# Late x1 rows fetched batch by batch in an AdaLN, feed-forward and mixture-of-experts kernel

## The reference, cut to what matters

```python
x = x + ffn0(adaln(x, cond))          # ternary weights, 8-bit activations, D_FF = 2048
y = causal_conv(x, taps)              # depthwise, 16 taps per channel (taps = cond)
logits = y @ Wr                       # 8 experts
w, sel = top_k(logits, 2)
w = softmax(w)
x = x + sum over e of gate[..., e] * (y @ We[e] + be[e])
```

## Time and profile before

| | |
|---|---|
| median of three runs | 834.71 us (832.91 to 834.76) |
| the profiled execution's own time | 831.19 us |
| its span | 829.2 us, 13313 instructions |
| TensorE matmul busy | 730.0 us, 88% |
| VectorE, ScalarE, GpSimd busy | 532.6, 436.9, 499.5 us |
| TensorE's mean granted clock | 0.948 of 2.4 GHz |

### The profile page before, as it was taken

One profiled execution on the slowest core, in us unless ns is written; L12 is line 12 of the kernel. 1 busy time (PEld: TensorE's weight loads), 2 busy tenths in 40 slices (PEclk: granted clock), 3 DMA queues, 4 the chain that ended last, 5 costly groups with the idle time before them and its releaser, 6 DMA issues.

```text
span 829.2 us, 13313 instructions
## 1 busy us (share of the span) xinstructions
PE 730.0 (88%) x3808; PEld 479.1 (58%) x3808; DVE 532.6 (64%) x765; ACT 436.9 (53%) x721; POOL 499.5 (60%) x760
## 2 busy tenths in 40 slices
PE   1754679999999999999999789984689999999995
PEld 0111235555555555655555479983568888888884
DVE  2467989889888888848975433684364544444442
ACT  2055466777777877658777423571343333333332
POOL 1036888777777787747862320011568888788773
PEclk9986899999999999989999988997689999999998
DMA  9985135656667766737656457799978989888883
GB/s 357 387 303 184 32 74 100 130 124 154 151 141 166 140 150 140 152 75 147 139 101 133 88 106 65 198 242 286 291 156 154 161 159 163 161 157 160 154 156 41
DMA packets 225049, 132.25 MB, mean 159 GB/s; under 512 B 182402, under 2 KB 186498, under 8 KB 223826
## 3 DMA queue, kind: packets, MB, share of 16 engines
q1 hardware_dynamic: 206866, 91.65, 46.5%
q0 software_dynamic: 15904, 35.48, 23.2%
q10 hardware_dynamic: 2208, 4.28, 1.7%
HBM read 74.44 MB, written 37.78 MB: 135 GB/s over the span
## 4 chain that ended last, share of the span: by engine, by line
PE 74%; DMA 9%; SPq 7%; DVE 4%; issue 3%; POOL 2%; ACT 2%; POOLq 0%; DVEq 0%; ACTq 0%
PE PS L1761 21%; PE PS L1595 12%; PE PS L1607 12%; PE PS L1618 12%; PE PS L1672 6%; PE PS L1743 3%; PE PS L1639 3%; SPq L424 3%; DMA z_scratch<-ZS 2%; SPq L509 2%; DMA WRT<-in_Wr 2%; PE PS L1648 2%; PE PS L1630 1%; DMA QyT<-Qy 1%; DMA X<-in_x 1%
## 5 line engine op out<-in xcount | busy, mean ns | idle before, releaser
L1761 PE MATMUL PS<-W,ZH 128*128 x568 | 187.6, 412 | 6.4 <-DVE W L1357 6.3
L1595 PE MATMUL PS<-W,QyT 128*128 128x512 bf16 x512 | 126.0, 391 | 26.4 <-DMA QyT<-Qy 16.2
L881 POOL DMA_INDIRECT out_x<-YS,IDS x71 | 114.1, 1606 | 43.7 <-issue 21.2
L1105 ACT ACTIVATE YS<-YS,SG 128x512 f32<-128x512 f32 x71 | 51.4, 724 | 150.5 <-DVE YS L1520 150.5
L1607 PE MATMUL PS<-W,QyT 128*128 128x512 bf16 x512 | 122.3, 382 | 0.0
L1761 PEld LDWEIGHTS PS<-W,ZH 128*128 128x128 f32 x568 | 104.8, 194 | 26.6 <-issue 7.7
L872 POOL DMA_INDIRECT ZR<-z_scratch,IDG x71 | 74.0, 1042 | 72.2 <-DVE IDG L1467 32.4
L1618 PE MATMUL PS<-W,QT 128*128 128x512 bf16 x512 | 116.8, 381 | 0.0
L1761 PE MATMUL PS<-W,ZL 128*128 x284 | 114.0, 401 | 0.0
L1499 DVE TENSOR_TENSOR ZL<-PS,ZH 128x512 fp32r<-128x512 f32 x71 | 49.1, 692 | 98.1 <-ACT ZH L1091 98.1
L942 ACT ACTIVATE SG<-PS,sm 128x1024 f32<-128x1024 f32 x64 | 71.3, 1114 | 60.1 <-PE PS L1595 60.1
(11 more groups left out here) (249 smaller groups left out, 1110.8 us busy)
## 6 DMA issues: line engine op xcount, KB each, us to landing
X<-in_x SPq DMA_DIRECT2D x32, 256.0 KB, 10.0
out_x<-X SPq DMA_DIRECT2D x32, 256.0 KB, 2.5
WRAW<-in_We SPq DMA_DIRECT2D x32, 256.0 KB, 9.0
ST<-out_x SPq DMA_DIRECT2D x28, 256.0 KB, 3.5
XR<-in_x SPq DMA_DIRECT2D x20, 256.0 KB, 3.5
z_scratch<-ZS SPq DMA_DIRECT2D x1, 4112.0 KB, 17.9
z_scratch<-ZS ACTq DMA_DIRECT2D x1, 4112.0 KB, 18.7
stage<-in_w1T SPq DMA_DIRECT2D x4, 1024.0 KB, 7.9
```

Of the source, the lines that this page charges most:

```text
L881: pool.indirect_dma_start(x1_d, bass.IndirectOffsetOnAxis(IDS[:, m:m + 1].bitcast(U32), 0), YS[m % UN][:], None, bounds_check=TOK - 1, oob ...
L1595: i = nc.tensor.matmul(GP[:, a, :], QyT[t][:, k, :], W12[:, k, o:o + CH], start=(k == 0), stop=(k == KD - 1))
L1761: x = nc.tensor.matmul(bank[i], zz[i % 2][:, k, :], W2[:, bass.ds(q, 1), part, k, :].rearrange("p o d -> p (o d)"), start=(k == 0 and n == ...
```

## The change

`stage_late(b)` now fetches one batch: b = 8 and 9 in stage 28, 10 and 11 in stage 29, 12 in stage 30, 13 in stage 31, each behind `stage_xw` and ahead of the g store. It has a counter of its own, stl_in. GpSimd copies STL into XW in stage 32, between the memset of BD 12:28 and that of BD 60:64, and no longer behind its constants of the routing. STL moves over PJ, so a batch waits for the last sums that read PJ (sum_done); STB moves over the Y tiles and, in its second use, over ION. The two last tap pieces are one, 44 to 64. The exponential stands behind the ZS copy of group 11. The waits on bd_zero are counted anew. The words "z stored whole" in the change's title have no line in the diff; `store_z` is as it was.

```diff
--- before.py
+++ after.py
@@ -144,8 +144,8 @@
         a += D // 2 * 5
         GAM = place("GAM", a, [P, D])
         BET = place("BET", a + D, [P, D])
-        STL = place("STL", a_s + 3 * D, [P, BH - 2, CB, NI - IL])
-        STB = place("STB", a_s + 5 * D, [P, CB, NI])
+        STL = place("STL", a_s + 5 * D, [P, BH - 2, CB, NI - IL])
+        STB = place("STB", a_h + OB * ZP, [P, CB, NI])
         TMP = place("TMP", a + 2 * D, [P, FF], I16)
         TMPB = place("TMPB", a + 2 * D, [P, FF], BF16)
         a += 2 * D + FF // 2
@@ -300,6 +300,7 @@
         pj_in = [sem(f"pj_in{t}") for t in range(2)]
         x1_out = [sem(f"x1_out{t}") for t in range(2)]
         st_in, xw_copied, xw_v = [sem(f"st_in{i}") for i in range(2)], sem("xw_copied"), sem("xw_v")
+        stl_in = sem("stl_in")
         z_out, z_free = [sem(f"z_out{h}") for h in range(2)], sem("z_free")
         ext_in = sem("ext_in")
 
@@ -343,7 +344,7 @@
         trz_done, zh_done, zl_done, exp_done, ys_done = (sem(n) for n in ("trz_done", "zh_done", "zl_done", "exp_done", "ys_done"))
 
         VM2 = 25
-        PIECES = [(0, 4), (4, 12), (12, IA), (IA, IB), (IB, IC), (IC, NI)]
+        PIECES = [(0, 4), (4, 12), (12, IA), (IA, IB), (IB, NI)]
         LATE_XW = 2 * (B - 2)
 
         def group(r):
@@ -486,13 +487,12 @@
                 sp.dma_start(ST[c][:], bass.AP(x1_d.tensor, b * S * D + c * (CB // 2) * OB * D,
                                                [[NI, P], [OB * D, CB // 2], [1, NI]])).then_inc(st_in[c], 16)
 
-            def stage_late():
-
-                sp.wait_ge(down_done, NT)
+            def stage_late(b):
+
+                sp.wait_ge(sum_done, NT - TB)
                 for t in range(TB):
-                    sp.wait_ge(x1_out[t], 16 * (B - 2))
-                sp.dma_start(STL[:].rearrange("p b k i -> p (b k) i"),
-                             bass.AP(x1_d.tensor, BH * S * D + IL, [[NI, P], [OB * D, (BH - 2) * CB], [1, NI - IL]])).then_inc(st_in[0], 16)
+                    sp.wait_ge(x1_out[t], 16 * b + 16)
+                sp.dma_start(STL[:, b - BH], bass.AP(x1_d.tensor, b * S * D + IL, [[NI, P], [OB * D, CB], [1, NI - IL]])).then_inc(stl_in, 16)
 
             def stage_last(b):
 
@@ -500,6 +500,8 @@
                     sp.wait_ge(x1_out[t], 16 * b + 16)
                 if b == B - 1:
                     sp.wait_ge(xw_v, 1)
+                else:
+                    sp.wait_ge(yint_done, NT)
                 sp.dma_start(STB[:], bass.AP(x1_d.tensor, b * S * D, [[NI, P], [OB * D, CB], [1, NI]])).then_inc(st_in[1], 16)
 
             def load_bd(i):
@@ -575,6 +577,8 @@
                     load_xr(s + 5)
                 if 4 <= s < NT:
                     stage_xw(s - 4)
+                for b in {28: (8, 9), 29: (10, 11), 30: (12,), 31: (13,)}.get(s, ()):
+                    stage_late(b)
                 if tile(s - 4) and s - 4 < NT - 1:
                     store_g(s - 4)
                 if 6 <= s <= 32 and s % TB == 0 and s != 22:
@@ -588,22 +592,16 @@
             pipeline(stage)
 
             load_gs(B - 2)
-            sp.wait_ge(bd_zero, 5)
+            sp.wait_ge(bd_zero, 6)
             sp.wait_ge(bd_zero_v, 3)
             sp.wait_ge(bd_in[0], 16 * NJ)
             load_bd(3)
             load_gs(B - 1)
             stage_last(B - 1)
-            sp.wait_ge(bd_zero, 6)
+            sp.wait_ge(bd_zero, 7)
             sp.wait_ge(bd_zero_v, 4)
             sp.wait_ge(bd_in[1], 16 * NJ)
             load_bd(4)
-            sp.wait_ge(bd_zero, 4)
-            sp.wait_ge(bd_in[2], 16 * NJ)
-            load_bd(5)
-            stage_late()
-            sp.wait_ge(x1t_done, NT)
-
             def load_expert(e):
 
                 if e >= E // 2:
@@ -796,6 +794,8 @@
                 if s == NT:
                     pool.wait_ge(hint_done, NT)
                     pool.memset(BD[:, 12:IA], 0.0).then_inc(bd_zero, 1)
+                    pool.wait_ge(stl_in, 16 * (BH - 2))
+                    pool.tensor_copy(XW[:, 1, IL:NI, 1:1 + CB, 0:BH - 2], STL[:].rearrange("p b k i -> p i k b")).then_inc(bd_zero, 1)
                     pool.wait_ge(xw_copied, LATE_XW)
                     pool.memset(XW[:, 1, IL:NI, 0, :], 0.0)
                     pool.memset(BD[:, IC:NI], 0.0).then_inc(bd_zero, 1)
@@ -856,8 +856,6 @@
             pool.memset(STEP[:, 5:6], 2.0)
             pool.memset(STEP[:, 7:8], 0.0).then_inc(route_p, 1)
 
-            pool.wait_ge(st_in[0], 16 * (LATE_XW // 2 + 1))
-            pool.tensor_copy(XW[:, 1, IL:NI, 1:1 + CB, 0:BH - 2], STL[:].rearrange("p b k i -> p i k b")).then_inc(bd_zero, 1)
             pool.wait_ge(ext_in, 48)
             pool.wait_ge(slots_done, 2)
 
@@ -1071,8 +1069,9 @@
                     copy_lg(1)
                 if r == 10:
                     act.wait_ge(route_v, 4)
+                    act.wait_ge(xw_v, 2)
                     nc.scalar.copy(ION[:], IOSB[:].rearrange("p (m o) -> p m o", o=1).broadcast_to([P, P, CC])).then_inc(route_e, 1)
-                if r == 12:
+                if r == 11:
                     act.wait_ge(route_v, VM2)
                     nc.scalar.activation(EX[:], M2[:], ACT.Exp).then_inc(route_e, 1)
                 if r in (20, 22, 24, 26):
@@ -1431,8 +1430,6 @@
                     dve.wait_ge(tab_done, q - 1)
                     dve.wait_ge(num_done, NUMS * (q - 1))
 
-                if q == 0:
-                    dve.wait_ge(bd_zero, 7)
                 nc.vector.tensor_tensor(BOX[h][:], over(IOSB, 0, MT), along(MTB, q, MT), ALU.is_equal).then_inc(boh_done, 1)
                 dve.wait_ge(boh_done, 2 * q + 1)
                 nc.vector.tensor_scalar(BOH[h][:, :, 1, :], BOX[h][:], PIDX[h], None, ALU.mult).then_inc(boh_done, 1)
@@ -1661,7 +1658,7 @@
                 if r == NG:
                     pe.wait_ge(xw_copied, LATE_XW)
                     pe.wait_ge(xw_v, 2)
-                    pe.wait_ge(bd_zero, 7)
+                    pe.wait_ge(bd_zero, 5)
                 if r < NG:
                     pe.wait_ge(bd_in[piece_of(g) % 3], 16 * NJ * (1 + piece_of(g) // 3))
                 if r >= 4:
```

## The result

| | before | after |
|---|---|---|
| median of 20 runs | 833.94 us (831.17 to 836.13) | 835.37 us (833.50 to 838.69) |
| ratio, after to before | | 1.0025, 95% interval 1.0015 to 1.0034 |
| the profiled execution | 831.19 us, span 829.2 | 838.69 us, span 836.6 |
| TensorE busy, mean granted clock | 730.0 us, 0.948 | 731.8 us, 0.939 |

A forecast was written before the change was run, and what follows sets the result against it. SyncE's queue, without a gap from 463.25, was taken to bound the hand-over to the convolution. Only stage 31 cost anything, +0.86 us, all other terms 0: 834.71 + 0.86 = 835.6 us, range 832.3 to 837.2.

The forecast's parts named there:

- Rival A: SyncE, stage 31: the issue behind a 2048-run load is stretched and moves the tap pieces, 835.6 us; chance 0.56.
- The surplus: SyncE's queue: extra time that each new 2048-run load puts on the issue behind it, taken as 0.95 us.
- the QyT row: SyncE, stage 28: QyT transpose behind a GS load takes 2.16 us to issue, against 1.21 the stage before.
- The cover: SyncE, stage 31: its wait ahead of piece 0 for VectorE's memset of BD 0 to 4, 0.72 us, absorbs added issuing.
- One sign of being wrong: TensorE, convolution: the forecast is wrong if the time from group 3 to the last group changes by over 0.5 us.
- The covers: Slack or idle time on the queues and engines that was to hold the change's other parts at cost 0.
- stages 28 to 30: SyncE's queue: added loads fit the slack between a transpose and its use a stage later; cost 0.
- the copy on GpSimd: GpSimd, stage 32: the 1.60 us copy fits ahead of 14 us of idle time; cost 0.
- the merged pieces: SyncE, last tap pieces: 8 issues fewer save 6 us of queue that nobody takes up; gives 0.
- Rival B: SyncE, stage 31: no stretch, or it falls into the wait; 0.63 us against 0.72 of cover, 834.7 us; chance 0.18.
- Rival D: SyncE, stage 31: queue stands behind batch 13 until it lands, +2.6 us, 837.3 us; or a counter holds an engine; chance 0.13.
- Rival C: TensorE, group 16: usually waits for the late load's copy; removing that wait makes it faster, down to 832.1 us; chance 0.13.

## Why the prediction was right

*The mechanism.* Rival A, the forecast, is what happens: a stretched issue behind batch 13, then tap pieces, groups 1 and 3, and the end. Taking that batch away takes the loss away, and leaving out the other parts does not.

*The sizes.* The forecast was +0.86 us and the median 835.6; measured are +1.4 by medians, +2.1 by the ratio (interval 1.3 to 2.8), and a median of 835.37. That the median came within 0.3 us is luck: that of before was taken 0.8 us too high, and the step 0.6 to 1.2 us too low. The surplus was taken as 0.95 us from the QyT row and is 1.20 (1.84 less 0.64). The cover, taken as 0.72 us, was too large by 0.09: without any wait SyncE still has a gap of 0.09 between the g store and piece 0. With 0.66 for the load and its gaps that gives 0.66 + 1.20 - 0.63 = 1.23, against 1.24 measured for the shift of piece 0. The rest was not in the sum at all. Over the four profiles with one batch in stage 31 group 3 starts at 28.04 us behind the memset in the mean, over the five with none and SyncE issuing alone at 26.48: +1.55 us. The column "rest" gives 82.15 against 80.49, +1.66, and here no profile of the one kind reaches those of the other (81.86 to 82.50, and 80.28 to 80.61). This lies in the intervals of all three kernels timed with one batch there.

*Where the sum stopped too early.* The prediction let piece 2 and group 3 move by what piece 0 moves. The start of piece 2 does (+1.22 us in the mean), its end does not (+2.15). Here are, in the kernel before, the last issue of piece 2 and the g store behind it; then, after, the sixth and the last issue of piece 2:

```profile
486.69 0.61 SPq L509 DMA_DIRECT2D BD<-taps_scratch  x1
...
487.98 0.96 SPq L519 DMA_DIRECT2D g_scratch<-GT  x1
```

```profile
488.37 0.61 SPq L511 DMA_DIRECT2D BD<-taps_scratch  x1
...
489.94 1.50 SPq L511 DMA_DIRECT2D BD<-taps_scratch  x1
```

In all nine profiles one issue that starts 23.3 to 25.0 us behind the memset is stretched by 0.4 to 0.9 us (with two batches in stage 31 it is the last of piece 2 again, at 26.0). Where piece 2 starts early, it falls in four of five profiles on a transfer behind the piece; where batch 13 has pushed piece 2 back by 1.2 us, it falls on one of its last two issues. (The fifth is the one with the pieces and the exponential alone, where it hits the last issue and piece 2 takes 6.90 us.) This is read from the profiles; no run changed it alone, and whether the stretched issue keeps its time or goes with the piece is not shown. Group 3 moves by only 0.3 us more than piece 0, so most of it doesn't reach TensorE.

*The signs.* The issue behind batch 13 was 1.84 us for 1.6, piece 0 came at 1.31 for 0.9. Group 1's wait was met almost exactly, 5.65 us for 5.7, but by luck: group 1 came 1.26 us later, not 0.86, and the work ahead of it ended 0.48 us later too. TensorE's rhythm and GpSimd's copy came as forecast. One sign of being wrong was set off: the time from group 3 to the last group changed by 1.22 us, and 0.5 was the limit. 0.73 of that is the clock of groups 9 to 14; the 0.47 ahead of the logits was missing in the sum, though in the mean of the profiles only 0.1 us is left of it. The prediction also counts three transfers between piece 1 and the x1 store of 478.20; the trace has two, and nothing hangs on it.

*Rows not read.* Stage 24 of the kernel before issues two GS loads in a row. Its rows show 2.88 us for the second load, at 382.71, and 2.92 for the QyT transpose behind it. They would have given a larger bound than a single GS does. And the x1 store behind the GS of stage 30, at 453.07, takes 0.37 us: a row without any surplus, though it starts 1.5 us after that GS issue has ended.

*The covers.* All held, but for the small wait of group 7: stages 28 to 30 (TensorE's down projections start at 438.76, 450.45 and 462.13, 11.69 apart), the copy on GpSimd, the merged pieces, the exponential, STB. *Rival B*: the late load is not free; in stage 31 its 2048 runs cost the next issue 1.2 us. The sentence of the Trainium skill (DMA: Bandwidth & Descriptors, Anatomy of one DMA) that many descriptors can be emitted before their cost shows is on the GpSimd path, and it doesn't carry over to SyncE's queue here. *Rival D*: the queue is not held until the batch has landed; piece 0 starts 2.54 us behind the issue of batch 13, and such a load takes 3.7 us to land. *Rival C*: no sign of it.

*Open.* What holds the queue, and what stretches the issue near the end of piece 2. The surplus is no fixed price either. It can fall on a transfer 4 us later; behind the GS of stage 28 the QyT transpose took 2.16 us before and takes 1.32 after, where late batches stand ahead of it; and behind batch 12 in stage 30 it is larger than behind batch 13, as the g store there shows (0.64 us before):

```profile
452.68 2.12 SPq L521 DMA_DIRECT2D g_scratch<-GT  x1
```

Why TensorE's clock comes back at different times behind the logits is open too.

## What to carry to other kernels

A queue that issues small DMAs back to back is an engine, and its time is to be read like one: find the moment from which it has no gap, and count what is added ahead of it. Moving work to an idle place gains nothing if the place that it left was covered as well, and one of six new pieces in the wrong stage is enough to lose. Before two profiles are compared over a stretch, look at the granted clock in it: here it moved the end of the convolution by up to 1.5 us between executions, as much as what was looked for. Where a queue is the bound, give part of its issues to an idle engine's queue.

## What the runs showed of the hardware that was not expected

On SyncE's queue the cost of a load with many runs is not in its own row (0.59 to 0.60 us for probes of 512 to 4096 runs) but in the next one, and it steps up between 1024 and 1536 runs: 0.62, 0.69 to 0.85, 1.91, 2.21, 2.68, 2.87 us for 512, 1024, 1536, 2048, 3072, 4096, one issue each. Cutting a load in two neither helped nor hurt in the one execution that shows it, as the second issue took up the surplus of the first. ScalarE's queue issued its four small transfers in 2.68 us beside SyncE's own four in 2.82; half of the 5.08 us for eight would be 2.54, so issuing side by side costs each little.
